# First edge layer: the comparisons between tiles move ahead of the statistics in VectorE's step

## The reference

```python
h = relu(layernorm(x))
messages = einsum('ni,rio->rno', h, weight)[edge_type, dst]      # 8 matrices of 256x256
x = x + relu(segment_sum(messages, src) + bias)                  # first edge layer
h = relu(layernorm(x))
h_neigh, h_self = h @ W_neigh, h @ W_self
msg = (h_neigh with all but its 32 largest per row set to 0)[src]
x = x + h_self + segment_sum(msg, dst) / max(degree(dst), 1)     # second edge layer
```

## Time and profile before

| | |
|---|---|
| median of 3 runs | 3609.3 us (3604.76 to 3609.43) |
| the profiled execution's own time | 3607.24 us |
| its span | 3605.5 us |
| busy in the span: DVE, PE, POOL, ACT | 87%, 72%, 68%, 63% |
| first edge layer, VectorE's steps 0 to 99 | about 311 to 1,712 us |
| mean gather and mean add instruction on POOL | 1,054 and 1,663 ns |

### The profile page before, as it was taken

One profiled execution on the slowest core, in us unless ns is written; L12 is line 12 of the kernel. 1 busy time (PEld: TensorE's weight loads), 2 busy tenths in 40 slices (PEclk: granted clock), 3 DMA queues, 4 the chain that ended last, 5 costly groups with the idle time before them and its releaser, 6 DMA issues.

```text
span 3605.5 us, 69112 instructions
## 1 busy us (share of the span) xinstructions
PE 2593.9 (72%) x10738; PEld 1677.9 (47%) x10739; DVE 3119.8 (87%) x13785; ACT 2257.1 (63%) x6394; POOL 2450.8 (68%) x1732
## 2 busy tenths in 40 slices
PE   2665666767788888888677777777777765766676
PEld 1224655555566666666333333333333334555454
DVE  8998788888899999999699999999999995666666
ACT  3994233333333333333588888888888867777787
POOL 0003877767787777777688888888888855656665
PEclk9997888888999999999899899998988988889999
DMA  9601466666555555555344444444444437777776
GB/s 368 248 0 48 83 123 144 147 143 149 110 108 104 104 100 103 105 102 100 109 173 164 182 166 171 178 163 177 173 164 182 166 121 244 257 242 258 247 251 218
DMA packets 308041, 576.38 MB, mean 160 GB/s; under 512 B 32095, under 2 KB 188034, under 8 KB 307982
## 3 DMA queue, kind: packets, MB, share of 16 engines
q1 hardware_dynamic: 212366, 419.40, 33.2%
q0 software_dynamic: 95616, 156.31, 22.3%
HBM read 316.70 MB, written 258.88 MB: 160 GB/s over the span
## 4 chain that ended last, share of the span: by engine, by line
DVE 50%; issue 21%; PE 11%; DMA 8%; POOL 4%; DVEq 3%; ACT 2%; POOLq 0%; ACTq 0%; SPq 0%
DVE zone_c L1176 7%; DVE w L1176 7%; DVE best L1169 6%; DVE zone_c L1204 5%; DMA agg<-msg,sidx 5%; PE banks L1569 5%; DMA w<-hs,gidx 3%; PE banks L1469 2%; DVE zone_c L858 2%; DVE zone_c L1049 2%; DVE zone_c L1047 2%; DVE stats L893 2%; DVE zone_c L860 2%; DVE zone_c L1051 2%; POOL rows_in L653 2%
## 5 line engine op out<-in xcount | busy, mean ns | idle before, releaser
L1541 PE MATMUL banks<-w,hT 128*128 128x512 f32 x1568 | 795.4, 666 | 199.8 <-ACT hT L1321 195.1
L665 POOL DMA_INDIRECT agg<-msg,sidx x400 | 665.3, 1663 | 206.4 <-issue 111.9
L653 POOL DMA_INDIRECT rows_in<-in_x,gidx x400 | 421.8, 1054 | 435.7 <-DVE gidx L909 305.3
L1541 PEld LDWEIGHTS banks<-w,hT 128*128 128x128 f32 x1568 | 325.7, 213 | 613.3 <-issue 500.6
L1204 DVE SCALAR_TENSOR_TENSOR zone_c<-banks,rdeg,zone_c 128x256 f32 x784 | 379.4, 484 | 245.8 <-PE banks L1569 201.0
L1569 PE MATMUL banks<-w,zone_c 128*128 x1568 | 428.1, 429 | 208.4 <-DVE zone_c L1204 99.5
L732 POOL DMA_INDIRECT w<-hs,gidx x392 | 371.3, 947 | 230.3 <-DMA w<-hs,gidx 90.6
L1411 PE MATMUL banks<-pick,h 128*128 128x128 f32 x1600 | 287.1, 307 | 311.8 <-ACT h L1220 218.8
L1469 PE MATMUL banks<-w,hT 128*128 x1600 | 481.1, 429 | 18.3 <-issue 17.1
L1238 ACT COPY msg<-banks 128x256 f32<-128x256 f32 x400 | 148.0, 370 | 510.6 <-PE banks L1480 497.3
L1569 PEld LDWEIGHTS banks<-w,zone_c 128*128 128x128 f32 x1568 | 316.1, 212 | 320.6 <-issue 275.2
(11 more groups left out here) (233 smaller groups left out, 5841.6 us busy)
## 6 DMA issues: line engine op xcount, KB each, us to landing
out_rows<-zone_c SPq DMA_DIRECT2D x196, 512.0 KB, 2.7
agg<-bias SPq DMA_DIRECT2D x2, 25344.0 KB, 97.3
zone_c<-agg SPq DMA_DIRECT2D x98, 512.0 KB, 5.4
hs<-zone_c SPq DMA_DIRECT2D x98, 512.0 KB, 3.6
zone_c<-out_rows SPq DMA_DIRECT2D x98, 512.0 KB, 6.0
rows_in<-in_x SPq DMA_DIRECT2D x97, 512.0 KB, 4.6
keyrow<-key_rows SPq DMA_DIRECT2D x100, 320.0 KB, 4.0
zone_c<-bucket_rows SPq DMA_DIRECT2D x28, 448.0 KB
```

Source lines behind the costliest of these rows:

```text
L653: pool.indirect_dma_start(out=rows_in[p][:, j, :], out_offset=None, in_=x[:, :], in_offset=bass.IndirectOffsetOnAxis(ap=gidx[p][:, j:j + 1 ...
L665: pool.indirect_dma_start(out=agg[:, :], out_offset=bass.IndirectOffsetOnAxis(ap=sidx[p][:, j:j + 1], axis=0), in_=msg[p][:, j * D:(j + 1) ...
L1541: last = mm(bank[4 + j][:, :], hT[p][:, c, j * P:(j + 1) * P], w1[:, c, :], start=(c == 0), stop=(c == KC - 1))
```

## The change

The part of `edge0_front` from the wait for the gathered rows on becomes a function of its own, `edge0_rows`, and VectorE's step calls it last but for the chunk: columns, `pick`, degree comparisons and `livekey` of group t, then `cross` and `sidx` of group t-1, then gathered rows, statistics and scales of group t.

```diff
                 v.tensor_tensor(livekey[p][:, :], extra[p][:, :], keycol[p][:, :], ALU.add).then_inc(live0, 1)
+
+            def edge0_rows(b, r, p):
                 dve.wait_ge(gathered0[p], 16 * B * (r + 1))
                 v.tensor_copy(gidx[p][:, :], from0[:, bass.ds(b * B + 2 * B, B)]).then_inc(staged0, 1)
                 statistics(b, p, rows_in, stats0, var0)
...
             def edge0_body(phase, at, chunk):
-                for part, lag in ((edge0_front, 0), (edge0_cross, 1), (edge0_back, 1)):
+                for part, lag in ((edge0_front, 0), (edge0_cross, 1), (edge0_back, 1), (edge0_rows, 0)):
```

## The result

The changed kernel takes 3636.7 us (median of 4 runs, 3630.0 to 3640.1) against 3608.2 for the kernel before in the same comparison: 1.0078 times as long, 95% interval 1.0060 to 1.0096. The forecast was +14.6 us and 3622; it is +28, about twice that, and 0.7 us above the upper end of the range.

A forecast was written before the change was run, and what follows sets the result against it. GpSimd's pace with its stalls was taken to bound hist and rank, VectorE the sort section; 0.6 + 0 + 11 + 1.1 + 0 + 1.9 = 14.6 us on 3607.24 gave 3622 us, range 3612 to 3636.

The forecast's parts named there:

- term 1: Start of the layer: add 1 of group 0 gets its message later, +0.6 us (0 to 1.9).
- term 2: Hist section: GpSimd runs without stalls before and after, 0 us, +-1.
- term 3: Rank section, some 27 steps: add 1 starts into SyncE's loads and add 3 waits, +0.4 us each, +11 us.
- As long as GpSimd sets the pace, lag is paid once, not per step: Hist and rank sections: VectorE's 1.9 us of lag behind GpSimd, from `met` waiting for add 4, does not recur each step.
- one example weighs less than 25: Rank section: group 26's stall costs 3.0 us against 1.8 per group now; 2.2 taken, a third of the way up.
- term 4: Into the sort section: step 43 is released by add 4 of group 40, +1.1 us, once (0 to 2).
- term 5: Sort section, 56 steps: `met` has 2.6 us of room, so 0 us, bounds +-5.
- term 6: End of the layer: `shift` of the last group comes later in step 99, +1.9 us (0.9 to 1.9).
- Rival A: Lag alone: the rank section's stall stays 1.8 us whichever add is hit; +3.6, 3611 us, chance 0.25.
- rival B: Faster: rank section's loads stall GpSimd by less than 0.9 us a group, 24 us go; 3587 us, chance 0.13.
- Rival C: Sort section: VectorE newly waits in each of 56 steps, 0.7 us each, +39; 3650 to 3660 us, chance 0.07.
- signs foretold: `met` waits in hist and rank, not sort; `gidx` wait gone; GpSimd stalls before add 3; rank 8 to 15 us longer.

The follow-up runs named there:

- rank_only: New order in the rank section's 30 steps alone, old order elsewhere, against the kernel before: 3616.0 against 3599.7 us, ratio 1.0045.
- second pair: Both kernels unedited, profiled again on other chips: before 3670.6 us where its median is 3667, changed 3690.9 against 3657.8, ratio 1.0096.
- sort_only: Old order in hist and rank, new order in the sort section and the steps behind it, against the kernel before: 3618.3 us, ratio 1.0051.

## Why the prediction was wrong

Two terms of the sum failed. The 0 for the sort section was wrong in both pairs of profiles (+6.4 and +7.0 us). The rank section's term had the right mechanism, but it left out what the entry costs and took the section for one steady state: +16.7 us in the first pair and +6.7 in the second, for +11. By the prediction's own steps:

1. Start of the layer (term 1), +0.6: step 13 started at 512.96 for 512.90. Hist (term 2), 0: as forecast in this pair.
2. Rank section (term 3), +11: measured +16.7 (438.9 to 455.6) in the first pair of profiles, +6.7 in the second, +16.3 timed in rank_only. The mechanism stands: `met` waits for add 4, add 1 starts into the loads, add 3 waits. GpSimd's stall grew by 0.7 us a group in the first pair (19.1 us over 27 groups), where the term had 0.4. The step that failed is "As long as GpSimd sets the pace, lag is paid once, not per step", with a price of nothing for that once. The lag was 1.9 us by the lone adds' 3.68 us; on entry loads caught add 1 and then add 4 itself, and VectorE stood 8.40 us. Step 15 costs 5.1 us more, step 14 1.9, step 38, where it stood 5.32 us, 4.5; the last four give 4.1 back. Of the rest, +0.4 a step was right on average (steps 16 to 36: 14.97 to 15.39), which is in part luck: it is a mean over two states of 14.2 and 15.7, which the sum did not have, and in the second pair the same steps are level (15.02 to 15.05). My "one example weighs less than 25" judged group 26's stall to be rare; it is that bad state, and the new order locks into it.
3. Into the sort section (term 4), +1.1: step 43 went from 18.9 to 21.0 us, +2.1, `met` waiting 4.59 for the add of 973.38 where 3.68 were reckoned from an earlier one.
4. Sort section (term 5), 0 within 5: measured +6.4 by profile, +7.0 in the second pair, and 17.5 between sort_only and the shortest sort section of the old order on the same chip. This term failed in both pairs. I had named it ("16-bit comparisons meet other instructions of GpSimd") and left it as a bound with the mean at nothing, without a reason for the nothing. Where instructions meet is not chance here: GpSimd's place in the step hangs on VectorE's own statistics, so a meeting repeats in most of the 55 steps.
5. End (term 6), +1.9: +1.6.

Sum of the first pair: 0.1 + 16.7 + 2.1 + 6.4 + 1.6 = 26.9 us (26.8 unrounded), against 14.6. In the second pair it is 20.6, of which 2.9 lie in the hist section, where 0 was forecast. Rival A (only lag) is refuted by rank_only, rival B (faster) by both timings of the changed kernel, though its rank steps of 14 us exist in the good state. Rival C (a new wait in each sort step) is refuted as worded: no wait came, the instructions themselves got longer. Of the signs foretold, most came: waits at `met` (33 times, 76.0 us in the whole span), none for rows at `gidx`, GpSimd's stalls before add 3 in the steps around step 22, and no wait for adds at `met` in the sort section. The rank section's growth of 8 to 15 us did not: it was 16.7, and 6.7 in the second pair.

The Trainium skill, "DMA: Bandwidth & Descriptors", section "Queues, rings and completion order", has each DMA engine take turns between queues. By the prediction's estimate from that rule taken alone, a caught add would land in 5.8 us. Caught by the whole burst it took 7.7 to 8.7 us in most steps of the changed kernel; only with the burst split did the chain show 5.76 and 6.46. This trace does not agree with the rule taken alone.

## What to carry to other kernels

Where two engines and a transfer queue release each other in a ring, moving a block changes which of them meet in every round. Ask not for the average stall but which state the ring settles in, what it costs to get there, and whether a start that two waits share (here one semaphore that lets 1.1 MB go) can be split; that was worth more than any order of VectorE's work. An instruction that is "only moved" can be slowed by another engine's instruction at a fixed distance, once per step. And where several states are possible, one profile need not be a kernel's typical execution.

## What the runs showed of the hardware

A 128x392 16-bit comparison on VectorE is held by about 0.3 us when it starts 0.5 to 0.7 us behind the start of a GpSimd indirect transfer instruction, and by 0.1 us at 1.2 us behind an add's. The Trainium skill, "SBUF — State Buffer", section "SBUF: two separate sides", has VectorE, in some kinds of its instructions, and GpSimd share a port pair that one of them holds for a whole instruction. The direction agrees. The length does not: the add's 1.58 us never held a comparison for more than about 0.3 us, and most comparisons inside it ran at full speed.

An add caught by SyncE's 1.1 MB mostly takes 7.1 to 8.7 us from start to landing in the two kernels, and 3.7 to 3.9 where it is not caught (the changed kernel's chain has both):

```profile
704.99 8.58 DMA agg<-msg,sidx
...
717.73 3.81 DMA agg<-msg,sidx
```
